# First layer's expert slots ordered by batch, with the first batch's next stage worked between them

## The reference, cut to what matters

```python
# layer 0: attention (one head), residual and layernorm, then
shared = silu(x @ shared_w1.T) @ shared_w2.T          # hidden 512
top2 of 8 experts by gate logits; gates = softmax of the two
selected = sum_k gate_k * (silu(x @ w1[e_k]) @ w2[e_k])
x = layernorm(x + shared + selected)
# layer 1: a state-space block
h = rmsnorm(x); xz = h @ W_in; x_in, z = split(xz)    # 256 channels each
x_act = silu(causal_conv4(x_in)); x_db = x_act @ W_x  # dt_lr, B, C (16 states)
delta = softplus(dt_lr @ W_dt + b_dt)
scan over 512 tokens:  state = exp(delta*A)*state + delta*x_act*B;  y = sum state*C
x = layernorm(x + x + (y*silu(z)) @ W_out)
# layer 1: mixture again: 8 gated experts, top 2, and a shared expert, then layernorm
```

## Time and profile before

| what | value |
|---|---|
| three runs | 633.61, 634.85 (median), 638.89 us |
| profiled execution | 632.36 us, span 630.6 us |
| busy share of the span | PE 85%, DVE 71%, POOL 60%, ACT 55% |
| mean granted TensorE clock | 0.954 |
| routing of layer 0, from the first count to the first slot | 79.4 to 98.7 us |
| 39 slots of layer 0 | 98.7 to 174.6 us |
| between the slots and POOL's first product of a state | 174.6 to 222.7 us |
| 64 states | 217 to 458 us |
| routing and slots of layer 1, and the end | 458 to 630.6 us |

### The profile page before, as it was taken

The page is one execution under the profiler, slowest core; times in us unless marked ns, Lnnn a source line. Parts: engine busy times, 40 slices in busy tenths (PEclk is TensorE's granted clock), DMA queues, the critical chain, the costliest instruction groups (busy, mean ns, idle before and its releaser), DMA issues.

```text
span 630.6 us, 9025 instructions
## 1 busy us (share of the span) xinstructions
PE 538.8 (85%) x3000; PEld 378.9 (60%) x3000; DVE 450.8 (71%) x966; ACT 349.8 (55%) x628; POOL 376.9 (60%) x308
## 2 busy tenths in 40 slices
PE   8988898999968298779777996898789899999985
PEld 5666576999954133235333532343348599999965
DVE  3445485555434799999997989999958766655627
ACT  3434564444413868955994499678423444544543
POOL 1011107745057797988897689789931576677640
PEclk9989999999989689889988998999999899999998
DMA  4252302768111533443344343444200111111124
GB/s 117 55 183 75 127 1 55 238 221 216 42 47 37 184 126 137 154 166 110 126 153 167 133 135 121 166 139 161 84 17 2 39 44 47 44 46 43 35 68 143
DMA packets 33245, 66.25 MB, mean 105 GB/s; under 512 B 6401, under 2 KB 20294, under 8 KB 32560
## 3 DMA queue, kind: packets, MB, share of 16 engines
q1 hardware_dynamic: 27136, 44.31, 21.5%
q0 software_dynamic: 4768, 9.32, 6.1%
q10 hardware_dynamic: 1296, 12.06, 5.3%
HBM read 57.60 MB, written 8.52 MB: 105 GB/s over the span
## 4 chain that ended last, share of the span: by engine, by line
PE 49%; POOL 15%; DVE 13%; issue 12%; ACT 5%; DMA 4%; POOLq 0%; SPq 0%; ACTq 0%; DVEq 0%
PE ps L835 6%; PE ps L689 6%; PE ps L693 6%; PE ps L701 5%; PE ps L725 5%; PE ps L717 5%; PE ps L772 4%; POOL w L1939 4%; POOL wide L1939 3%; DVE wide L1791 2%; DVE work L1499 1%; DVE w L1791 1%; DVE ps L1784 1%; POOL nT_all L1977 1%; POOL work L1901 1%
## 5 line engine op out<-in xcount | busy, mean ns | idle before, releaser
L2006 POOL DMA_INDIRECT rows<-xn_rows,source x78 | 78.0, 1000 | 71.1 <-DVE place L1514 22.1
L1791 DVE TENSOR_TENSOR_SCAN wide<-work,ps 128x512 f32<-128x512 f32 x86 | 99.7, 1201 | 2.2 <-ACT work L1238 2.2
L835 PE MATMUL ps<-wide,ident 128*128 128x512 f32 x128 | 66.4, 644 | 20.8 <-POOL wide L1939 20.7
L1784 DVE TENSOR_TENSOR ps<-ps,w 128x512 f32<-128x512 f32 x128 | 81.5, 683 | 1.1 <-DMA w<-bc_rows 1.1
L835 PE MATMUL ps<-w,ident 128*128 128x512 f32 x124 | 64.7, 651 | 14.3 <-POOL w L1939 14.3
L1238 ACT ACTIVATE work<-work,a_neg 128x512 f32<-128x512 f32 x86 | 56.6, 711 | 11.2 <-DVE wide L1791 9.7
L1939 POOL TENSOR_TENSOR wide<-wide,w 128x1024 f32<-128x1024 f32 x22 | 51.8, 2356 | 13.3 <-DVE wide L1791 13.0
L835 PEld LDWEIGHTS ps<-wide,ident 128*128 128x128 f32 x128 | 24.0, 200 | 57.5 <-POOL wide L1939 35.2
L1564 DVE TENSOR_TENSOR wide<-wide,ps 128x512 f32<-128x512 f32 x39 | 26.8, 687 | 42.5 <-PE ps L693 41.5
L835 PEld LDWEIGHTS ps<-w,ident 128*128 128x128 f32 x124 | 23.9, 202 | 49.7 <-POOL w L1939 26.1
L1939 POOL TENSOR_TENSOR w<-wide,w 128x1024 f32<-128x1024 f32 (+1 forms) x21 | 48.9, 2329 | 8.2 <-DVE wide L1791 8.0
(11 more groups left out here) (322 smaller groups left out, 1229.1 us busy)
## 6 DMA issues: line engine op xcount, KB each, us to landing
w<-bc_rows SPq DMA_DIRECT2D x64, 512.0 KB, 3.7
w<-in_w ACTq DMA_DIRECT2D x2, 2304.0 KB, 9.3
wg<-in_wg ACTq DMA_DIRECT2D x1, 2304.0 KB
wu<-in_wu ACTq DMA_DIRECT2D x1, 2304.0 KB
wd<-in_wd ACTq DMA_DIRECT2D x1, 2304.0 KB
w<-y_choice SPq DMA_DIRECT2D x8, 256.0 KB, 4.4
y_slots<-yout SPq DMA_DIRECT2D x20, 64.0 KB, 2.3
rows<-xn_rows,source POOLq DMA_INDIRECT x78, 2.7
```

The lines of the kernel that those rows point to most:

```text
L835: last = mm_(bank(6 + h), ident[:, :], hc[j % 4][:, h, :], start=False, stop=(j == NS - 1))
L1784: V.tensor_tensor(dbu[:, h, :], du[:, h, :], bc_all[j % 4][:, 0:S], ALU.mult).then_inc(dbu_set, 1)
L1791: V.tensor_tensor_scan(st[n % 3][:, h, :], dA[n % 3][:, h, :], dbu[:, h, :], 0.0, ALU.mult, ALU.add).then_inc(st_set if h else st_half, 1)
L2006: G.indirect_dma_start(out=xin[i % RING][:, :], out_offset=None, in_=xn_rows, in_offset=bass.IndirectOffsetOnAxis(ap=source[:, i:i + 1], a ...
```

## The change

The first layer's rows are placed by batch first and expert second. For this the counts are taken at the end of each batch (`held_by`, `own_rows`, `ends`, `offs`, `jump`), and a row's position is moved by what the batches before leave (`moved`). Batch 0 is complete with slot 15, batch 1 with slot 23, batch 2 with slot 31 (`READY`). The expert of each slot is now counted with one slot in each partition and turned by a small product on PE (`experts`). The second layer uses the same code with one group.

The down products of batches 2 and 3 move ahead of the slots. In PE's list the taps follow the slots 3 and 7, and batch 0's turn, convolution and projections follow the slots 31 to 37. POOL fetches batch 0's tiles after the gathers 26 and 30, batches 1 and 2 after the last gather, and batch 3 between the states (0,4) to (0,7) and (1,0) to (1,3). DVE adds batch 0's tiles in steps 19, 21, 24 and 26, batch 1's in 36 and 37. For batch 1 `norm_group` stands after `first_step`. Batch 0 and 1's fetched rows lie in `wd`, whose load moves from slot 22 to state (0,2). In batch 1 of the states `add_rows` moves from state 3 to 7, `late_scales` from 7 to 10, `added_stats` from 6 to 9, and `scale_fetched` from 2 to 5.

```diff
-        LOAD_AT = {4: (wg, "wg"), 13: (wu, "wu"), 22: (wd, "wd")}
+        LOAD_AT = {4: (wg, "wg"), 13: (wu, "wu")}
+        GROUPS = ((0, 1, 2, 3), (3,))
+        READY = [((b + 1) * 2 * S + NE * (P - 1)) // P for b in range(NB)]
+        JOIN_AT = (19, 21, 24, 26)
...
@@ PE: moe
-                    pe.wait_ge(*sT_set[0].at(NB * HB))
+                    shared_down(0, 2)
+                    shared_down(0, 3)
@@ PE: step(i)
+                    if i == 3:
+                        spread_taps()
+                    if i == 7:
+                        spread_bias()
+                    if i == 31:
+                        turn_xn(0)
+                    if i in (32, 33):
+                        convolve(0, 0, (2 * (i - 32), 2 * (i - 32) + 1))
+                    if i in (34, 35):
+                        convolve(0, 1, (2 * (i - 34), 2 * (i - 34) + 1))
+                    if i == 35:
+                        project_z(0, 0)
+                    if i == 36:
+                        project_low(0)
+                        project_z(0, 1)
+                    if i == 37:
+                        project_dt(0)
@@ ACT: step(i)
+                    if i == 8:
+                        act.wait_ge(taps_ps, 3)
+                        cp(w_dt[DTR:DTR + 1, :], ps[DTR:DTR + 1, 3, 0:EI]).then_inc(bias_set, 1)
+                    if i == 30:
+                        scale_rows(0)
+                    if i == 31:
+                        take_xnT(0)
+                    if i == 34:
+                        activate(0, (0,))
+                    if i == 35:
+                        activate_z(0, (0,))
+                    if i == 36:
+                        activate(0, (1,))
+                    if i == 37:
+                        take_low(0)
+                        activate_z(0, (1,))
+                        act.preload_act_table(ACT.Exp)
@@ ACT: states(b)
+                    if (b, j) == (0, 2):
+                        act.wait_ge(*var_set[0].at(2))
+                        act.dma_start(wd[:], a["wd"]).then_inc(ld_f1, 16)
-                    if (b, j) in ((0, 1), (1, 2)):
+                    if (b, j) in ((0, 1), (1, 5)):
                         scale_fetched(b + 2)
@@ DVE: routing
-                    link(V.tensor_tensor(pos[:, :, :], pos[:, :, :], over_t(offs[:, :]), ALU.add))
+                    moved = (eq, posk, late)
+                    for g in range(1, n):
+                        own, shp = slice(g * QT, NT), [P, NT - g * QT, NE]
+                        to = moved[g - 1][:, own, :] if g < 3 else late[:, :, :]
+                        steps.mark(V.tensor_tensor(to, pos[:, own, :], held_by[:, g, :].unsqueeze(1).to_broadcast(shp), ALU.is_ge))
...                     # then times jump, plus offs of the first batch, plus each of the three
@@ DVE: step(i)
+                def between_slots(i):
+                    if i in (0, 1):
+                        add_base(0, 2 + i)
+                    if i == 5:
+                        make_taps()
+                    if i in JOIN_AT:
+                        combine_tile(JOIN_AT.index(i))
+                    if i == 27:
+                        variances(0, 0)
+                    if i == 29:
+                        pull_mean(0, 0)
+                    if i == 31:
+                        norm_group(0)
+                    if i in (36, 37):
+                        combine_choice(1, i - 36)
+                    if i == 38:
+                        take_stats(1)
+                        variances(0, 1)
@@ POOL: moe, after gather i
+            def between_gathers(i):
+                if i == 26:
+                    pool.wait_ge(*idx_set[0].at(2))
+                    slots_stored(0)
+                    fetch_two(0)
+                    fetch_two(1)
+                if i == 30:
+                    fetch_two(2)
+                    fetch_two(3)
+                if i == 35:
+                    inverse_group(0, 0)
+                if i == ROUTED - 1:
+                    for b in range(1, NB - 1):
...
+                        slots_stored(b)
+                        for t in range(b * QT, b * QT + QT):
+                            fetch_two(t)
@@ POOL: states(b)
-                    if (b, j) in ((0, 2), (1, 3)):
+                    if (b, j) in ((0, 2), (1, 7)):
                         add_rows(b + 2)
-                    if (b, j) in ((0, 6), (1, 7)):
+                    if (b, j) in ((0, 6), (1, 10)):
                         late_scales(b + 2)
+                    if b == 0 and 4 <= j < 8:
+                        fetch(3 * QT + (j - 4) // 2, j % 2)
+                    if b == 1 and j < 4:
+                        fetch(3 * QT + 2 + j // 2, j % 2)
```

More of the change, by code:

```diff
@@ L183, in area @@
             return v
-        past = area(11792, ROUTED, NE)
+        ends, offs, own_rows = (area(11792 + k * NB * NE, NB, NE) for k in range(3))
+        jump, late, passed = area(11888, NB - 1, NE), area(11912, QT, NE), area(11944, NB * NE)
+        cnt_i = area(11976, NB, NE).bitcast(I32); slot_ei = area(12008, ROUTED).bitcast(I32)
         own_d = [area(DOWN_AT + k * HID, HID) for k in range(2)]
@@ L202, in build @@
         y_k = [w1[:, k * T:(k + 1) * T] for k in range(2)]
+        y_first = [wd[:, k * 2 * S:(k + 1) * 2 * S] for k in range(2)]
         all_stats = sb("all_stats", [P, NT, 6]); all_mv = sb("all_mv", [P, NT, 2])
@@ L791, in project_dt @@
                         pe.wait_ge(bc_set, x + 1)
-                    last = mm_(bank(LOOSE[h]), w_dt[:, h * P:(h + 1) * P], dts[:, :], start=True, stop=True)
+                    last = mm_(bank(side(x)[h]), w_dt[:, h * P:(h + 1) * P], dts[:, :], start=True, stop=True)
                 last.then_inc(dl_ps, 1)
@@ L927, in states @@
                         add_up(b * NS + (j - 2), j - 2)
-            turn_xn(0)
-            for h in range(EH):
-                convolve(0, h)
-            project_z(0, 0)
-            project_low(0)
-            project_z(0, 1)
-            project_dt(0)
+            moe(0)
             for b in range(NB):
@@ L1182, in soft_parts @@
                 for h in range(EH):
[L1183 removed]
+                    steps.mark(A(u1[:, h, :], bank(side(x)[h]), ACT.Abs))
                 act.wait_ge(act_step, steps.n)
@@ L1478, in routing @@
                     dve.wait_ge(*counts_taken[l].at(1))
-                    link(V.tensor_tensor(pos[:, :, :], pos[:, :, :], over_t(offs[:, :]), ALU.add))
+                    moved = (eq, posk, late)
[3 more added lines that the diff above has]
+                        steps.mark(V.tensor_tensor(to, pos[:, own, :], held_by[:, g, :].unsqueeze(1).to_broadcast(shp), ALU.is_ge))
+                    dve.wait_ge(dve_step, steps.n)
+                    for g in range(1, n):
+                        own, shp = slice(g * QT, NT), [P, NT - g * QT, NE]
+                        to = moved[g - 1][:, own, :] if g < 3 else late[:, :, :]
+                        steps.mark(V.tensor_tensor(to, to, jump[:, g - 1, :].unsqueeze(1).to_broadcast(shp), ALU.mult))
+                    link(V.tensor_tensor(pos[:, :, :], pos[:, :, :], over_t(offs[:, 0, :]), ALU.add))
+                    for g in range(1, n):
+                        own = slice(g * QT, NT)
+                        to = moved[g - 1][:, own, :] if g < 3 else late[:, :, :]
+                        link(V.tensor_tensor(pos[:, own, :], pos[:, own, :], to, ALU.add))
                     for k in range(2):
```

269 lines of the change are left out of this document (152 added, 117 removed).

## The result

The changed kernel takes 642.04 us in the median of 8 runs (637.12 to 644.11), the kernel before 635.09 (633.61 to 639.42, 8 runs). The ratio is 1.0089, 95% interval 1.0049 to 1.013: slower by 0.9%, by more than the measurement is uncertain. The forecast was 634.7, no change, in a range of 625 to 644. The profiled execution took 643.56 us with a span of 641.6; the one before took 632.36 with 630.6. So 11.0 us are to be found in the trace.

The account below looks back on a forecast made before the run. PE was taken to bound the slots, DVE with POOL close behind the states, a chain the hollow. Terms -5.4 + 2.7 + 1.1 + 0.6 + 1.0 = 0.0 left 632.4 profiled, median 634.7, range 625 to 644.

Parts of the forecast that it names:

- Routing, +2.9: Layer 0's routing, ahead of the first slot: added small DVE operations make the one-hots, and PE's table, 2.9 us later.
- The two down products, +7.2: Moved from the hollow to between PE's last up products and the first slot, the pair takes 7.2 us back to back.
- Bulk loads: Second load during the slots, third during states 3 to 6: each delays small transfers, priced at 0.5 us each.
- slower* rival: Bulk load delays slot 14's store, gathers come late, PE stands 3.5 to 8 us in the slots: 644, chance 0.20.
- lead of the ring: In the slots, POOL's gathers are 15 us ahead of PE; a lead of 5 us was to cover the loads' delays.
- PE's inserts and new waits, +15.2 and +3.7: PE in the slots: 33 instructions and four transposes lengthen them 15.2; waits at steps 36 and 37 plus turn add 3.7.
- DVE and POOL between the slots, 0: In the slots, DVE's additions taken as 0 (upper bound 5); POOL's early fetches, up to 10 us, hidden by the ring.
- From dt to the first state, 11.0: Behind the slots, from dt to DVE's first product of a state: 11.0 us instead of 9.0, first state at 211.6.
- Batch 3's fetches +2.7, add_rows +1.1: In the states: fetches at 6 and 7 cost batch 0 +2.7, batch 1 absorbs all four; moved add_rows nets +1.1.
- The sign that I had given for this: In the states: POOL without idle time from state 6, DVE waiting 3 to 4 us before L1721 in both batches.
- Layer 1, +0.6 and 0.5 for the third load: Layer 1's routing gains small operations, +0.6 us; the third bulk load, meeting B and C loads in the states, 0.5.
- Descriptors locked out, 0.03: Rival: DVE's copies in the slots hold up POOL's 24 fetches, 10 us later, mostly hidden: +2, 636.7, chance 0.03.

Follow-up runs that it names:

- c2: Changed kernel with bulk loads at steps 0 and 6, batch 3's fetches ahead of the states, add_rows, scales and statistics back at their old states: 679.01 us, ratio 1.0253.
- e3: Changed kernel with only batch 3's eight fetches moved on POOL from inside the states to ahead of them: 684.19 us, one run.

## Why the prediction was wrong

The prediction had most of the mechanisms and took the wrong side of one. By its own steps:

- **Routing, +2.9.** The one-hots end at 95.68 instead of 92.61, +3.07. Right.
- **The two down products, +7.2.** They took 7.31 with the clock at 1.00. Right. But the first slot is 2.8 late against the forecast, 2.55 of it because of the up products of L565 ahead of them: 6.22, where I had carried over 3.67 from the earlier trace rows. The one-hots now come later than PE's other work, PE stands idle twice, and the products behind that ran at the 1.2 GHz level. I had no term for the clock after a wait.
- **Bulk loads, "I take 0.5 for each".** This is the step that failed. The median landing of 2.6 leaves out most of the stores behind a load: the view has a landing only where all records of a ring place stand, for 19 of the 39 stores. Its maximum, 10.8, is a store issued 0.3 us behind a load. Slot 14's own store stood in the trace of before, 2.1 us behind the load of `wu`, with its last record after 7.9. In the changed kernel it took 9.3 and the price was 6.7. That is the *slower* rival's cause, and within its 3.5 to 8 us of standing PE, but not its path: it had PE waiting for gathered rows in slots 27 to 33. The ring hid POOL's lateness, and PE waited for no gathered row. It stood in slot 22 for DVE, whose first addition (step 19) waited for the fetch with the next copy of `xT` behind it. The term for DVE between the slots, 0, and the lead of the ring that the 0.5 leaned on had left this path out; that the price fell into the rival's bounds is partly luck. Moving the load took this stall away.
- **PE's inserts and new waits, +15.2 and +3.7.** Two of the waits came as told, 0.85 and 2.17 for 1.1 and 2.3. The inserts I haven't taken apart. dt and the last down product took 5.4 instead of 3.0 at a clock of 0.53: +2.4 that was not in the sum. That in eight other traces the same wait left dt's products at 1.95 or 1.96 says that this term is one of chance, not a fixed price.
- **DVE and POOL between the slots, 0.** Apart from the stall, right.
- **From dt to the first state, 11.0.** It was 11.2 (210.88 to 222.08). Right. The first state came at 222.08 instead of 211.6. Against it the terms above make 2.8 + (6.7 - 0.5) + 2.4 = 11.4, and with the load's own 0.5 in the forecast it is 10.0 late; the other 1.4 came back: 0.7 between the first slot and the end of dt (100.9 against 93.4, with 6.7 and 1.5 on top), and 0.7 behind dt, whose 11.2 holds the 0.86 of the down product.
- **Batch 3's fetches +2.7, add_rows +1.1.** The states lost 3.3 + 3.3 + 0.7. The fetches cost 2.4 in batch 0, near the forecast, and 2.0 in batch 1, where I had all four absorbed; the moved work 1.5 for 1.1. POOL has no idle time to absorb them from 247 us on. The sign that I had given for this, a wait of DVE of 3 to 4 us before the gate sum in both batches, did not come: it was 2.26 and 1.66. A large part of the loss lay before that, in DVE's waits for the loads of B and C, which are issued when POOL is done with a ring place: six waits and 5.3 us in all, against 1.1 in the kernel before, and in batch 0 3.1, against 0.96 in `c2`. The idle time was elsewhere: 20.8 us ahead of its first product, where the eight fetches (10 us) fit, and where `e3` puts them.
- **Layer 1, +0.6 and 0.5 for the third load.** From the third gate sum to the end it was 1.4 us less. The load of `wd` is free, as `c2` shows.
- **Descriptors locked out, 0.03.** POOL's 24 early fetches took 940, 944 and at most 1,237 ns beside DVE's copies of 128x512, as its gathers did before:

```profile
L2096 POOL DMA_INDIRECT wd<-y_slots,place x16: 940/944/1237, 153.3 to 190.3; - x16
L2096 POOL DMA_INDIRECT nT_all<-y_slots,place x8: 940/944/1015, 191.8 to 200.6; - x8
```

The Trainium skill (SBUF — State Buffer, section "Who interferes with whom") holds, of the ports of SBUF, that TensorE never waits on anyone. By that rule a port is not what made 115.9 us of 85.5 with the doubled gathers; no run here shows what did.

In sum, against the forecast: the load 6.2, the first slot 2.8, dt and the last product 2.4, what lies behind the first state 1.0, and 1.4 back: 11.0. What followed dt up to the first state came as forecast; most of the loss lay ahead of it.

## What to carry to other kernels

When a wait is moved up to a place beside a bulk load, price the transfer that it waits for by the row of a transfer issued as far behind such a load, and not by the median; follow every engine that waits for it, and what stands behind that wait in its list; then move the load, which is one edit. When work is moved into an engine's full stretch, ask where that engine is idle instead: POOL stood for 20.8 us ahead of the states while the fetches lay in its full list. A change that brings many indirect transfers beside dense PE work should be timed on more than one chip.

## What the runs showed of the hardware

- In two traces of the kernel before, batches 0 to 2 of the states took 63.4, 62.9 and 60.3 us to 0.01, while the kernel took 632 us in one and 658.5 in the other.
- Where the kernel takes 658 to 665 us, doubling POOL's gathers beside the slots took 663 products from 85.5 to 115.9 us (one run), though PE waited only 2.6 us for gathered rows.
- The same two waits of 1.4 and 1.5 us on PE were followed by eight products of 3.67 us in two traces and of 4.68 to 6.22 in six.
- 64 KB stores issued 0.3 and 2.2 us behind a load of 2,304 KB on another queue landed after 10.5 and 9.3 us, about when the load ended; with the load issued earlier the second took 1.5.
